# A graph network layer on one core: second layers with features on partitions, the product turned back by two transposes

## What is computed

```python
nodes = x[[src, dst]].reshape(E, 128)
gates = (ssp(edge_attr @ We1 + be1) @ We2 + be2) * (1 - sigmoid(5 * (dist - 3.5)))
h = ssp(nodes @ Wn1 + bn1) @ Wn2 + bn2        # ssp(x) = softplus(x) - log 2
message_sum = zeros(N, 64).at[dst].add(h * gates)
new = x + (ssp(message_sum @ Ws1 + bs1) @ Ws2 + bs2)
out = layernorm(x + new)
```

## Time and profile before

| | |
|---|---|
| median of 3 runs | 1991.86 us (1990.89 to 1994.37) |
| span of the profiled execution, its own time | 1988.8 us |
| TensorE (PE) busy | 1737.7 us, 87% |
| ScalarE (ACT) busy | 1532.1 us, 77% |
| GpSimd (POOL) busy | 1484.7 us, 75% |
| VectorE (DVE) busy | 1285.6 us, 65% |

### The profile page before, as it was taken

One profiled execution on the slowest core, in us unless ns is written; L12 is line 12 of the kernel. 1 busy time (PEld: TensorE's weight loads), 2 busy tenths in 40 slices (PEclk: granted clock), 3 DMA queues, 4 the chain that ended last, 5 costly groups with the idle time before them and its releaser, 6 DMA issues.

```text
span 1988.8 us, 53540 instructions
## 1 busy us (share of the span) xinstructions
PE 1737.7 (87%) x16249; PEld 1328.7 (67%) x16249; DVE 1285.6 (65%) x3512; ACT 1532.1 (77%) x3368; POOL 1484.7 (75%) x1572
## 2 busy tenths in 40 slices
PE   4699999898888988878889988998988898988987
PEld 3577777676666666666666766766666676766666
DVE  4578888666665655555656666666666666666666
ACT  3589999777777777777777788788777787787877
POOL 7777777777777777777777777777777777777773
PEclk7799999999999899999989999899999899999999
DMA  5433333333333333333333333333333233333331
GB/s 122 122 85 98 97 97 97 85 85 76 91 74 73 71 73 70 75 68 71 74 71 74 74 80 74 74 75 78 74 75 75 69 84 75 75 78 75 75 76 38
DMA packets 256432, 157.78 MB, mean 79 GB/s; under 512 B 45401, under 2 KB 227046, under 8 KB 256366
## 3 DMA queue, kind: packets, MB, share of 16 engines
q1 hardware_dynamic: 202652, 104.94, 18.2%
q0 software_dynamic: 50048, 51.35, 15.5%
q10 hardware_dynamic: 3666, 0.68, 0.2%
HBM read 146.94 MB, written 9.87 MB: 79 GB/s over the span
## 4 chain that ended last, share of the span: by engine, by line
POOL 57%; issue 22%; PE 11%; DVE 3%; ACT 2%; SPq 2%; DMA 2%; DVEq 1%; ACTq 1%; POOLq 0%
POOL ga L459 57%; PE ps L623 3%; PE ps L636 3%; PE ps L640 1%; DVE hid L1113 1%; SPq L340 1%; PE ps L585 1%; DMA ga<-in_x_dram,srcT 1%; PE ps L575 1%; DVE hid L1117 1%; PE ps L653 1%; PE ps L662 1%; PE ps L577 0%; DVEq L1139 0%; ACT lg L861 0%
## 5 line engine op out<-in xcount | busy, mean ns | idle before, releaser
L459 POOL DMA_INDIRECT ga<-in_x_dram,srcT x1564 | 1483.7, 949 | 477.6 <-issue 472.4
L852 ACT ACTIVATE lg<-ps,bn1c 128x512 f32<-128x512 f32 x391 | 268.4, 687 | 306.6 <-PE ps L585 267.6
L636 PE MATMUL ps<-wn,hid 128*128 128x64 f32 x3128 | 447.9, 288 | 18.9 <-DVE hid L1117 17.1
L1113 DVE SCALAR_TENSOR_TENSOR hid<-ps,neg_b,lg 128x512 f32<-128x512 f32 x391 | 292.8, 749 | 221.9 <-ACT lg L867 205.2
L636 PEld LDWEIGHTS ps<-wn,hid 128*128 128x128 f32 x3128 | 393.1, 197 | 51.5 <-DVE hid L1117 26.6
L575 PE MATMUL ps<-ident,ea 128*128 128x128 f32 x782 | 173.8, 305 | 198.2 <-DMA ga<-in_x_dram,srcT 135.2
L844 ACT COPY xe<-ps 128x512 f32<-128x512 f32 x391 | 229.9, 588 | 113.3 <-PE ps L577 99.8
L623 PE MATMUL ps<-xe,wn 64*128 64x256 f32 x1564 | 289.8, 449 | 0.0
L1151 DVE TENSOR_TENSOR acc<-acc,ps 64x64 f32 x782 | 168.4, 215 | 163.7 <-issue 157.9
L640 PE MATMUL ps<-we,hid 128*128 128x128 f32 x1564 | 273.1, 299 | 0.0
L575 PEld LDWEIGHTS ps<-ident,ea 128*128 128x128 f32 x782 | 80.0, 143 | 282.1 <-issue 268.8
(11 more groups left out here) (124 smaller groups left out, 1847.9 us busy)
## 6 DMA issues: line engine op xcount, KB each, us to landing
ea<-in_edge_attr_dram SPq DMA_DIRECT2D x195, 256.0 KB
ga<-in_x_dram,srcT POOLq DMA_INDIRECT x1564
bw<-b_tab SPq DMA_DIRECT2D x782, 32.0 KB
relb<-rel_tab SPq DMA_DIRECT2D x196, 64.0 KB
b_tab<-share SPq DMA_DIRECT2D x25, 250.0 KB
out_dram<-xs SPq DMA_DIRECT2D x25, 125.0 KB
xs<-in_x_dram SPq DMA_DIRECT2D x3, 750.0 KB
rows_i<-in_dst_dram SPq DMA_DIRECT2D x1, 768.0 KB
```

The costliest lines, as they stand in the source:

```text
L459: pool.indirect_dma_start(to[:, t % 2, t // 2, :], None, x, bass.IndirectOffsetOnAxis(ap=idx[:, t:t + 1], axis=0)).then_inc(done, 16)
L636: pe.matmul(hg[:, t * D:(t + 1) * D], hid[:, u % 2, t * P:(t + 1) * P], wn2[:, :], start=False, stop=False, skip_group_check=True)
L852: act.activation(lg[:, u % 2, 0:QUAD].rearrange("p (k e) -> p k e", k=2), z[:, :, 0:PAIR], ACT.Abs, bias=bn1c[:, 0:1]).then_inc(n_abs, 1)
L1113: dve.scalar_tensor_tensor(out=hid[:, u % 2, 0:QUAD].rearrange("p (k e) -> p k e", k=2), in0=ps[:, 2 * (u % 2):2 * (u % 2) + 2, 0:PAIR], s ...
```

## The change

`mid` now puts the features on partitions: the weights `Wn2` and `We2` are loaded and the hidden units are streamed past them. Two matmuls with 64 output partitions and 256 columns each make the nodes' part, four of 64 x 64 by 128 columns the edges' part. `gates_out` on ScalarE adds the gate's bias on its way to SBUF (128 x 256), `product` on VectorE adds the other bias and multiplies, `turn_back` on TensorE transposes the product by two transposes, and `message` multiplies by the cutoff, edges on partitions again. `fill`, `gcut` and the biases' replicated tiles go.

```diff
-        ps_hg = [ps[:, 6, :], ps[:, 5, :]]
+        ps_hid = [ps[:, 5 + n, PAIR:2 * PAIR] for n in range(2)]
+        ps_gate = [ps[:, 5:7, n * P:(n + 1) * P] for n in range(2)]
+        ps_m = ps[:, 7, P:P + PAIR]
...
+            for j in range(2):
+                half = slice(j * D, (j + 1) * D)
+                pe.matmul(ps[half, 7, 0:D], wn2[:, :], shift[:, 0, 0:D], start=True, stop=True)
+                pe.matmul(ps[half, 7, D:2 * D], we2s[:, :], shift[0:D, 1, 0:D], start=True, stop=True)
             pe.matmul(ps[:, 7, 2 * D:3 * D], shift[0:D, 2, :], ws2[0:D, :], start=True, stop=True).then_inc(bias_mm, 1)
...
-            for hg in ps_hg:
-                mm = pe.matmul(hg, ident[:, :], bsum[:, :, :, :].rearrange("p h k d -> p (h k d)"), start=True, stop=True)
-            mm.then_inc(hg_set, 1)
...
-            def mid(q, u, hg):
+            def mid(q, u, n):
 
                 pe.wait_ge(hid_b, q + 1)
-                pe.wait_ge(filled, q + 1)
-                for t in range(4):
-                    pe.matmul(hg[:, t * D:(t + 1) * D], hid[:, u % 2, t * P:(t + 1) * P], wn2[:, :],
-                              start=False, stop=False, skip_group_check=True)
-                gates = hg[:, PAIR:2 * PAIR].rearrange("p (k j d) -> p k j d", k=2, j=2)
+                if reached(q, 1):
+                    pe.wait_ge(prod_b, q)
+                units = hid[:, u % 2, 0:QUAD].rearrange("p (k j e) -> p j k e", k=2, j=2)
                 for j in range(2):
-                    mm = pe.matmul(gates[:, :, j, :], hid[:, u % 2, QUAD + j * P:QUAD + (j + 1) * P],
-                                   we2[:, :].rearrange("p (k d) -> p k d", k=2),
-                                   start=False, stop=(j == 1), skip_group_check=True)
+                    pe.matmul(ps_hid[n][j * D:(j + 1) * D, :].rearrange("d (k e) -> d k e", k=2), wn2[:, :], units[:, j],
+                              start=True, stop=True)
+                for k in range(2):
+                    half = slice(k * D, (k + 1) * D)
+                    for j in range(2):
+                        mm = pe.matmul(ps_gate[n][j * D:(j + 1) * D, k, :], we2[half, half],
+                                       hid[half, u % 2, QUAD + j * P:QUAD + (j + 1) * P], start=True, stop=True)
                 mm.then_inc(hg_mm, 1)
+
+            def turn_back(q):
+
+                pe.wait_ge(prod_b, q + 1)
+                if reached(q, 1):
+                    pe.wait_ge(msg_b, q)
+                for k in range(2):
+                    mm = pe.transpose(ps_m[:, k * P:(k + 1) * P], prod[:, k * P:(k + 1) * P], ident[:, :])
+                mm.then_inc(prod_t, 1)
...
                     transposes(s + 2, (v + 2) % ARING)
+                if not known or s >= 2:
+                    turn_back(s - 2)
                 if not known or s >= 3:
                     back(s - 3, (u - 3) % RING)
                 if not known or 1 <= s <= NQ:
-                    mid(s - 1, (u - 1) % RING, ps_hg[(u - 1) % 2])
+                    mid(s - 1, (u - 1) % RING, (u - 1) % 2)
...
                     front(s, s % ARING, group_at(s) if s < NQ - 1 else None)
                     if TAIL0 < s < NQ - 1:
                         transposes(s + 1, (s + 1) % ARING)
+                    turn_back(s - 2)
                     back(s - 3, (s - 3) % RING)
-                    mid(s - 1, (s - 1) % RING, ps_hg[(s - 1) % 2])
+                    mid(s - 1, (s - 1) % RING, (s - 1) % 2)
                 back(NQ - 3, (NQ - 3) % RING)
                 pe.wait_ge(flushed, NQ - 1 - BACK)
                 node_hidden(NG - 2, ps_h_end)
-                mid(NQ - 1, (NQ - 1) % RING, ps_hg[(NQ - 1) % 2])
+                turn_back(NQ - 2)
+                mid(NQ - 1, (NQ - 1) % RING, (NQ - 1) % 2)
                 back(NQ - 2, (NQ - 2) % RING)
                 node_out(NG - 2, ps_y_end)
+                turn_back(NQ - 1)
                 back(NQ - 1, (NQ - 1) % RING, ps_s_end)
...
-            for h, v in enumerate((bn2, be2)):
-                act.dma_start(brow[:, h, :], row(v).broadcast_to([P, D])).then_inc(ld_b, 16)
+            for n, v in enumerate((bn2, be2)):
+                for j in range(2):
+                    act.dma_start(bias2[j * D:(j + 1) * D, n:n + 1], col(v)).then_inc(ld_b, 16)
...
-            def fill(q, hg, ring):
-
-                if reached(q, ring):
-                    act.wait_ge(msg_b, q - (ring - 1))
-                act.copy(hg, bsum[:, :, :, :].rearrange("p h k d -> p (h k d)")).then_inc(filled, 1)
+            def gates_out(q, n):
+
+                act.wait_ge(hg_mm, q + 1)
+                if reached(q, 1):
+                    act.wait_ge(prod_b, q)
+                act.activation(gate[:, :].rearrange("p (k e) -> p k e", k=2), ps_gate[n], ACT.Identity,
+                               bias=bias2[:, 1:2]).then_inc(gate_e, 1)
...
                 logs(q, u)
-                fill(q, ps_hg[u % 2], 2)
+                if not isinstance(q, int) or q >= 1:
+                    gates_out(q - 1, (u - 1) % 2)
...
                     if TAIL0 < q < NQ - 1:
                         evacuate(q + 1, (q + 1) % RING)
+                    gates_out(q - 1, (q - 1) % 2)
                     logs(q, q % RING)
-                    fill(q, ps_hg[q % 2], 2)
                     if node is not None:
                         node_step(*node)
+                gates_out(NQ - 1, (NQ - 1) % 2)
                 node_sizes(NG - 2, ps_h_end)
                 node_log(NG - 2)
...
-            def message(q, u, hg, scattered=sc_mm):
-                dve.wait_ge(hg_mm, q + 1)
-                dve.tensor_tensor(gcut[:, u % 2, :].rearrange("p (t d) -> p t d", d=D),
-                                  hg[:, PAIR:2 * PAIR].rearrange("p (t d) -> p t d", d=D),
-                                  cutT[:, quad_cols(q)].unsqueeze(2).broadcast_to([P, 4, D]),
-                                  ALU.mult).then_inc(gc_b, 1)
-                dve.wait_ge(gc_b, q + 1)
-                if scattered is not None:
-                    if reached(q, 2):
-                        dve.wait_ge(scattered, q - 1)
-                dve.tensor_tensor(msg[:, u % 2, :, :].rearrange("p t d -> p (t d)"), hg[:, 0:PAIR],
-                                  gcut[:, u % 2, :], ALU.mult).then_inc(msg_b, 1)
+            def product(q, n):
+
+                dve.wait_ge(gate_e, q + 1)
+                if reached(q, 1):
+                    dve.wait_ge(prod_t, q)
+                dve.scalar_tensor_tensor(out=prod[:, :], in0=ps_hid[n], scalar=bias2[:, 0:1], in1=gate[:, :],
+                                         op0=ALU.add, op1=ALU.mult).then_inc(prod_b, 1)
+
+            def message(q, u, scattered=sc_mm):
+
+                dve.wait_ge(prod_t, q + 1)
+                if scattered is not None and reached(q, 1):
+                    dve.wait_ge(scattered, q)
+                dve.tensor_tensor(msg[:, u % 2, :, :], ps_m.rearrange("p (t d) -> p t d", d=D),
+                                  cutT[:, quad_cols(q)].unsqueeze(2).broadcast_to([P, 4, D]), ALU.mult).then_inc(msg_b, 1)
...
-                    message(s - 2, (u - 2) % RING, ps_hg[(u - 2) % 2])
+                    product(s - 2, (u - 2) % 2)
                 if node is not None:
                     node_step(*node)
                 if not known or s + 2 < NQ:
                     pick(s + 2, (u + 2) % RING)
+                if not known or 2 <= s <= NQ + 1:
+                    message(s - 2, (u - 2) % RING)
...
-                message(NQ - 2, (NQ - 2) % RING, ps_hg[(NQ - 2) % 2])
-                hidden(NQ - 1, (NQ - 1) % RING)
                 one_hot(NQ - 1, (NQ - 1) % RING)
                 flush(NQ - 3, 0)
+                product(NQ - 2, (NQ - 2) % 2)
+                hidden(NQ - 1, (NQ - 1) % RING)
+                message(NQ - 2, (NQ - 2) % RING)
+                product(NQ - 1, (NQ - 1) % 2)
                 node_hidden(NG - 2)
-                message(NQ - 1, (NQ - 1) % RING, ps_hg[(NQ - 1) % 2])
+                message(NQ - 1, (NQ - 1) % RING)
```

More of the change, by code:

```diff
@@ L148, in gnn_layer @@
         bmean = sb("bmean", [P, 1])
-        brow = sb("brow", [P, 2, D])
-        bsum = sb("bsum", [P, 2, 4, D])
+        bias2 = sb("bias2", [P, 2])
         rows_i = sb("rows_i", [P, 2, RG, QUAD], I32)
@@ L191, in gnn_layer @@
         hid = sb("hid", [P, 2, QUAD + PAIR])
-        gcut = sb("gcut", [P, 2, PAIR])
+        gate = sb("gate", [P, PAIR])
+        prod = sb("prod", [P, PAIR])
         msg = sb("msg", [P, 2, 4, D])
@@ L253, in gnn_layer @@
         s_rel = {k: sem(f"s_rel{k}") for k in range(0, RING, 2)}
-        xe_t, xe_e, oht_b, oh_b, z_mm, n_abs, e_abs, n_exp, e_exp, z_ln, hid_b, hg_mm, gc_b, msg_b, sc_mm, flushed = (
+        xe_t, xe_e, oht_b, oh_b, z_mm, n_abs, e_abs, n_exp, e_exp, z_ln, hid_b, hg_mm, gate_e, prod_b, prod_t, msg_b, sc_mm, flushed = (
             sem(n) for n in ("xe_t", "xe_e", "oht_b", "oh_b", "z_mm", "n_abs", "e_abs", "n_exp", "e_exp", "z_ln", "hid_b",
```

(26 more changed lines are left out.)

1 line of the change is left out of this document (removed).

## The result

The changed kernel takes 2007.3 us (median of 4 runs, 2006.6 to 2009.7), the kernel before beside it 1993.1: a ratio of 1.0071 (95% interval 1.0058 to 1.0083), 14.2 us slower. The forecast was 2012, with a range of 2003 to 2022.

A forecast was written before the change was run, and what follows sets the result against it. GpSimd's gathers bound the kernel, plus the end behind them; 12.4 (loop) + 0.4 (node_add) + 0.2 (logs(382)) + 1.65 (end) = 14.7, plus 5 for the clock = 19.7 us, forecast 2012 us, range 2003 to 2022.

The forecast's parts named there:

- The bound: GpSimd's row of 1564 gathers, 5.02 us a quad, runs as before; last gather within 2 us of 1963.
- rivals 2 and 4: 2: body itself becomes the bound, 2030 us, chance 0.11; 4: gathers come closer together, 1980 us, chance 0.03.
- TensorE's blocks: TensorE's step: mid 0.91 us in place of 1.54, turn_back adds 0.22, step 3.54 in place of 3.95.
- rival 3: mid's column halves run one behind the other: 4.2 us over the loop, 2016 us; shares the forecast's 0.75.
- The steps up to 381: Loop through four engines walked once in two steps; stays under the gathers' 5.02 us, so GpSimd runs as before.
- The sum of 4.03 us: Steps up to 381: 8.05 us for two steps, 4.03 a step against 3.95 before.
- The loop of steps 382 to 390: gates_out(q - 1) ahead of logs(q): 5.55 us a step against 4.00, 12.4 more; node_add 0.4, logs(382) 0.2 later.
- Rival 1: Steps 382 to 390: loop does not close, mid(q - 1) always done before gates_out; 1994 us, chance 0.06.
- The end: From logs(390) to back(390): 6.48 us in place of 4.83, 1.65 more, at full clock.
- The clock: TensorE partly at 1.2 GHz in the last steps: 1.25 us for each step at half clock, 5 us taken.
- "half": Last eight steps: none at half clock is 0, all are 10 us; half taken, 5 us.

The follow-up runs named there:

- the other execution: Changed kernel with turn_back(390) and back(390) ahead of node_out(23), message(390) ahead of node_hidden(23): 2005.0 us, ratio 1.0064.
- the added matmuls: Changed kernel plus matmuls whose result nobody reads, in TensorE's idle time in the last steps and the end: 2006.7 us, ratio 1.0054.
- the end built anew: Changed kernel with three reorders, plus hidden(390) ahead of product(389) and node_hidden(23) with its log ahead of quad 390's back half: 1997.8 us, ratio 1.0012.

## Why the prediction was right

**The bound.** The gathers kept their pace and their end, as forecast; rivals 2 and 4 fall with that.

**TensorE's blocks.** mid's node part takes 0.54 to the next block (1980.78 to 1981.32), for 0.53 forecast; rival 3's 1.06 falls. The gates 0.38 and turn_back 0.37 as forecast. back, followed by a block of its own shape, takes 0.28 and not 0.38.

**The steps up to 381.** The sum of 4.03 us was wrong for the steps with shares: 5.03 measured. It followed one loop through four engines and left out that message(q) waits for back(q - 1) as well, and that VectorE then does shares, centring and the load of places in its own order. It was wrong for the steps behind them as well: from 104 to 170, with neither shares nor node work and the transposes still behind, so that no gather holds them, a step takes 4.5 us, and every fourth one, behind the load of four pairs of places, takes 5.45 or more where the others take 3.4 to 4.6 (one of them 5.13). The forecast came out unhurt because the gathers allow 5.02. Both kernels are over 40 us behind the gathers by step 9; the kernel before works this off by step 72, the changed one, at just the gathers' pace, keeps it (48 us at most) until step 96 and is rid of it by step 190. A ring of about 75 us (15 steps of 5.02) covers that, as the prediction said of cover in general. That the steps with shares came out at 5.03 and not well above it was luck: the sum gave no reason for it.

**The loop of steps 382 to 390.** Right in kind and nearly in size: 5.55 forecast, 5.44 measured, which is back's 0.28. At full clock it costs 43.91 - 32.02 = 11.9 us where 12.4 + 0.4 stood; opening it gave back 11.9. Rival 1 falls: gates_out(q - 1) waits 1.5 and 2.4 us for mid(q - 1) in the rows above. logs(382) came 0.45 us earlier, not 0.2 later, which is within what the executions differ by.

**The end.** 6.48 us forecast from logs(390) to back(390), 6.54 measured at full clock, 7.52 as it runs.

**The clock.** The term that was mis-sized: 5 us taken, "half" of eight steps at 1.25, and about 2.1 measured, 1.1 in the steps and 1.0 at the end. The end's share was not in the sum at all; the steps' share was over four times too high (two and a half times against the 2.0 of the other execution), since TensorE was granted 2.4 GHz in most of them. The "half" had no row behind it. The Trainium skill (TensorE: Matmul & The Clock Gate, Part 1) has activity lift the clock; the trace agrees in direction (1.00 with the added matmuls, 0.87 to 0.88 without).

So 19.7 forecast against 15.6: 2.9 of the 4.1 too many are the clock in total, 0.9 the loop, 0.65 logs(382), and 0.35 went the other way behind back(390).

## What to carry to other kernels

On engines with one fixed order each, follow the product of one item through all of them and count how many steps the circle lies in: a circle of 5.5 us that must be walked once a step bounds the step, though no engine is busy for more than 4.2, and exchanging two lines on one engine opens it. Look for such circles in the first and last steps above all, where the order is often another than in the loop and no ring of buffers covers it. A piece of other work may stand where it does because it fills a wait: moved ahead it delayed the chain, moved behind it delayed it later, and TensorE came out of the hole that it left at half clock.

## What the runs showed that was not expected

A change of shape between two blocks on TensorE costs about 0.10 us by this pair of rows: back (8 records of 128 x 64) takes 0.28 us to the next block if that is mid in the same shape (1980.50 to 1980.78), and 0.38 if it is another. With back ahead of turn_back there is one change more among the three blocks back, turn_back and mid's node part, and they take 1.34 us in place of 1.19, 0.15 more. The Trainium skill (TensorEngine Tiling, Key Properties) says that a change of mode drains the engine; the runs are in line with it and give the change this size here.

The loads of places from SBUF into VectorE's registers stand in no row as busy, but hold its queue: 1.3 to 1.6 us for four pairs ("issue" ahead of L1174 at 208.51), 0.67 for three (ahead of hidden(390) with the end built anew), under 0.1 for one (one_hot to flush in eight of the nine last steps, 0.69 in the other). Loaded by fours they cost more here than one at a time.
